# The order of work in a two-block attention kernel: from a planner that looks ahead to written strings

## The reference

```
attn = softmax((q / |q|) @ (k / |k|).T * exp(min(logit_scale, ln 100)) + bias[rel_index])
h = relu(gn1(x + proj(attn @ v)));  z = relu(gn2(h + mlp(gn(h))))
```

```
attn = softmax(q.T @ k * 16 ** -0.5);  out = w_proj @ (attn @ v) + z
```

## Time and profile before

| what | us |
|---|---|
| median of three runs | 9722.46 |
| the profiled execution | 9728.87 |
| its span, first to last instruction | 9726.9 |
| TensorE (PE) busy in it | 8771.4 |
| VectorE (DVE) busy in it | 7528.1 |
| ScalarE (ACT) busy in it | 6459.0 |
| GpSimd (POOL) busy in it | 834.0 |

### The profile page before, as it was taken

How to read it: one execution, slowest core, us unless ns; L and a number is a source line. 1 busy time by engine, 2 the same in 40 slices (tenths; PEclk the granted TensorE clock), 3 DMA queues, 4 the chain that set the end, 5 groups by cost and what they waited for, 6 DMA issues and landing times.

```text
span 9726.9 us, 373040 instructions
## 1 busy us (share of the span) xinstructions
PE 8771.4 (90%) x145926; PEld 4275.9 (44%) x145926; DVE 7528.1 (77%) x9622; ACT 6459.0 (66%) x13874; POOL 834.0 (9%) x676
## 2 busy tenths in 40 slices
PE   4799999999999999999999999999999999999997
PEld 2344444444444444444444444444444444444443
DVE  3677887777787787887778877777877878877785
ACT  1466676676766667666666766767666676666777
POOL 3000100101000000000001001010000000000000
PEclk8799999999999999999999999999999999999999
DMA  1201102020020201102011020100202011020110
GB/s 29 42 10 23 30 6 45 10 37 16 9 42 8 43 11 22 29 7 44 10 22 31 6 44 10 33 20 9 42 8 43 11 21 31 7 44 10 22 23 18
DMA packets 123195, 225.77 MB, mean 23 GB/s; under 512 B 57218, under 2 KB 89090, under 8 KB 121354
## 3 DMA queue, kind: packets, MB, share of 16 engines
q1 hardware_dynamic: 121490, 201.52, 11.5%
HBM read 67.50 MB, written 42.73 MB: 11 GB/s over the span
## 4 chain that ended last, share of the span: by engine, by line
PE 71%; DVE 12%; DMA 5%; SPq 5%; issue 4%; ACT 3%; DVEq 0%; POOL 0%; ACTq 0%; POOLq 0%
PE PS L1210 20%; PE PS L1351 20%; PE PS L1363 19%; DVE small L991 7%; PE PS L1251 3%; PE PS L1271 2%; SPq L696 2%; DMA q_stack<-neg_rows 2%; DVE small L1030 1%; ACT exps L929 1%; SPq L725 1%; PE PS L1303 1%; DVE win_scores L1033 1%; PE PS L1312 1%; DMA tok_unit<-in_query_ident 1%
## 5 line engine op out<-in xcount | busy, mean ns | idle before, releaser
L929 ACT ACTIVATE exps<-PS 128x392 f32<-128x392 f32 x12800 | 5656.2, 499 | 2602.4 <-PE PS L1351 2089.2
L991 DVE TENSOR_REDUCE small<-PS 128x1 f32<-128x784 f32 x6400 | 5912.9, 966 | 964.4 <-PE PS L1210 775.6
L1351 PE MATMUL PS<-q_stack,k_stack 99*32 99x392 bf16 x51200 | 3802.0, 338 | 181.7 <-DMA q_stack<-neg_rows 85.0
L1210 PE MATMUL PS<-k_stack,q_stack 96*32 96x392 bf16 x51200 | 3497.5, 353 | 300.8 <-DVE small L991 194.9
L1363 PE MATMUL PS<-exps,v_all 128*32 128x392 f32 x25600 | 2740.7, 500 | 34.9 <-DVE o_st L1151 27.5
L1351 PEld LDWEIGHTS PS<-q_stack,k_stack 99*32 99x32 bf16 x51200 | 1461.7, 97 | 1845.9 <-ACT exps L929 1030.4
L1210 PEld LDWEIGHTS PS<-k_stack,q_stack 96*32 96x32 bf16 x51200 | 1210.7, 99 | 2020.5 <-DVE small L991 1148.6
L1363 PEld LDWEIGHTS PS<-exps,v_all 128*32 128x32 f32 x25600 | 802.3, 111 | 331.4 <-issue 62.0
L829 POOL TENSOR_TENSOR win_scores<-win_scores,small 128x784 f32<-128x784 f32 x256 | 384.5, 1502 | 3917.4 <-DVE small L1042 3917.4
L1030 DVE TENSOR_REDUCE small<-PS 128x16 f32<-128x784 f32 x256 | 247.2, 966 | 369.2 <-PE PS L1251 369.2
L1251 PE MATMUL PS<-kmask,tok_unit 113*64 113x392 f32 (+1 forms) x2048 | 399.5, 513 | 77.3 <-DMA tok_unit<-in_query_ident 69.6
(11 more groups left out here) (113 smaller groups left out, 3030.9 us busy)
## 6 DMA issues: line engine op xcount, KB each, us to landing
q_stack<-tok_qk SPq DMA_DIRECT2D x320, 98.0 KB, 3.7
k_stack<-tok_qk SPq DMA_DIRECT2D x320, 98.0 KB, 4.2
kmask<-tok_unit SPq DMA_DIRECT2D x1024, 12.2 KB
att<-scratch_att SPq DMA_DIRECT2D x68, 196.0 KB
z_half<-scratch_z SPq DMA_DIRECT2D x34, 392.0 KB, 5.8
inv_sums<-scratch_rden SPq DMA_DIRECT2D x272, 49.0 KB, 2.1
out<-inv_sums SPq DMA_DIRECT2D x68, 196.0 KB, 2.7
scratch_att<-o_st SPq DMA_DIRECT2D x512, 26.0 KB
```

Source lines behind the costliest of these rows:

```text
L929: nc.scalar.activation(exps(u), PS[:, u % SCORE_BANKS, 0:GTOK], ACT.Exp, scale=D1 ** -0.5).then_inc(s_exps, 1)
L991: nc.vector.tensor_reduce(max_parts[:, n_:n_ + 1], slot(), op=ALU.max, axis=AX.XY)\
L1210: last = mm(PS[32 * r:32 * r + 32, it.bank + j, 0:GTOK], q_stack[0:STACK, stage // 2, q0:q0 + 32], k_stack[0:STACK, stage // 2, chunk * GT ...
L1351: last = mm(PS[32 * r:32 * r + 32, u % SCORE_BANKS, 0:GTOK], k_stack[0:STACK + SHIFT, h, k0:k0 + 32], q_stack[0:STACK + SHIFT, h, c * GTOK ...
```

## The change

The walk that tries and looks ahead (earliest_unit, Walk, start, arrange) is gone. TensorE's list is written down as a string of letters for the prologue, the loop image and the last image. `follow` reads it: TensorE takes the next letter's step, SP, ScalarE, VectorE and GpSimd what is ready first in the walk, and for VectorE a part that empties a slot before another. Costs are in ns and differ a little. LEAD is 18, so 70 maxima stand in the prologue and 330 in the last image; the loop image keeps 400. The steps, their instructions and their semaphore waits are as before. The new loop string has 116 changes of tile shape. The diff, cut: of PARTS and LAST_ORDER only the beginning or end, of the functions removed only their names.

```diff
 PARTS = {
-    "score": (("PE", 17),), "exp": (("ACT", 41),), "weigh": (("PE", 69),),
-    "max": (("PE", 34), ("DVE", 90)), "shift": (("PE", 25), ("DVE", 16), ("SP", 25)),
-    "copy": (("DVE", 51),), "store": (("SP", 32),),
...
+    "score": (("PE", 167),), "exp": (("ACT", 380),), "weigh": (("PE", 664),),
+    "max": (("PE", 334), ("DVE", 884)), "shift": (("PE", 160), ("DVE", 220), ("SP", 2260)),
+    "copy": (("DVE", 560),), "store": (("SP", 1240),),
+    "xload": (("SP", 1100),), "xorder": (("POOL", 500),),
...
-SHIFT_PIECES = 140
-TAIL = {"PE": 20, "DVE": 18, "ACT": 18, "POOL": 15, "SP": 350}
-LATE = {"stack": 1200, "xload": 800, "sums": 1500, "zload": 1500, "rden": 600, "rspread": 700}
-AHEAD, PATIENCE = 600, 40
-SWITCH, URGENT = 10, 7
+SHIFT_PIECES = 1400
+TAIL = {"PE": 225, "DVE": 140, "ACT": 165, "POOL": 110, "SP": 3500}
+LATE = {"stack": 5000, "xload": 4000, "sums": 5500, "zload": 9000, "rden": 3500, "rspread": 3000, "zstore": 4000,
+        "kload": 2500, "queries": 2500, "shift": 3000}
+SWITCH = 100
...
-MAX_LOW, MAX_START, MAX_RATE = 4, 6, 2.0
-
 MAXIMA = [(stage, tile, pair) for stage in range(STAGES) for tile in range(*STAGE_TILES[stage % 2])
           for pair in range(PAIRS)]
 MAX_INDEX = {m: n for n, m in enumerate(MAXIMA)}
 STAGE_MAXIMA = [[m for m in MAXIMA if m[0] == stage] for stage in range(STAGES)]
-LEAD = 6
+LEAD = 18
 LEAD_IN = STAGE_MAXIMA[0] + STAGE_MAXIMA[1][:LEAD]
 
...
-def earliest_unit():
...
-class Walk:
...
-    def work(self, until):
...
-def start(needs, maxima, attended, last_slots):
...
+LETTERS = {"s": "score", "W": "weigh", "M": "max", "H": "shift", "q": "qk", "u": "sum", "p": "spread", "k": "wscore",
+           "v": "wval", "t": "wtrans", "o": "wpv", "j": "wproj", "g": "gn", "a": "mlp1", "b": "mlp2", "z": "gqk",
+           "y": "gv", "F": "final"}
+PROLOGUE_ORDER = (
+    "qqqquppvkkttkkopttokkvttkkotptkkotvtjkkottjkkovttjkkottojggggaaaabbaaaabbggzzzzyyyMMMMMMMMMMMMMMMMMMMMMMMMMMMMMM"
+    "MMMMMMMMMMMMMMMMMMMMMMMMMMMMMHMMMMMMMMMMM")
+IMAGE_ORDER = (
+    "MssMsMsssMWssMsMssWMssMssMWMsssMsMssWMMssWsssMsMssWMsMssWMsssMsMWMsssMsMWMsssMsqqqqsssMWMsMMsssWuMMWMMsssHMsssWs"
+    "WssppssMWssMMsssMWMssMsssMssMWMsvskkWssspsssWMsWsssMstWMsssMstkksssWWoMMsssMsssWMstWsMsstkkssssWoMMssWssMsstvsss"
+    "MWMsstkksssWWMssMsssMWosssMMsWsMssstMssWsMktWsssMksssWssMWMsssossMWMsssMsWMssstMWsssMMssWsMssMssWMssMsWssMMsWsss"
+    "psssMWHssMssMWMsssjksWsssMWMssstssMWMsssMWMsskvWjsssMssostMssWMMWssMssMsstkksssWWsMsMsssMWMsssMMsssMWMsssWMsssMW"
+    "ssMsosssMtssMWMMWsMsstMssWMkkssWsssvWsssMssossMMsWttssMWoMsMsssMMsWMsjsjsssMsWMMsWgssMsMssWssWsgssMHsssMMsssWWMM"
+    "sssMsssMWMsssMssMWWMsssFMssWsMssMssMWgsssMMssWgsMssMWMsssMssMWssMMsWsMMsMssMssMWMWMsssMMsssMWsMssaassMsMWMMsssMW"
+    "MsssMWMsssMWMsssMMWsMsMsMsssMWMsssbssWsMsMWMsssaassWHMsssaasWsMMsWsssMMsWsssMbsMssWMsssMWMsssMsMsWMsMsssWsMMsssW"
+    "sMssMsWMsssMWMssMssMsssMWMsMssWMssMWMsssaassMWMsssMWMssMssWMsssMWMssbbsssMWssMsMWsssgMsssMWMMsssMsWsssWsMssMWMss"
+    "MsssMWgssHsMssMWssMMsWMsssMMssWssMMsssWMsszzssWMsssMWMMsssMsWsMssMsWMssMsWssMssMWsssMMssWMsssMWssMsMssWssMMsssWM"
+    "ssMWsMssMWsMMsssMWssMMssWMsssMMsssMWsMssMWsMssMWMssMssssWsssMsMWsMssMsWMsssMWMssMssMWMsssMsszzsssWWMyHsssMMssWMs"
+    "ssMWsssMMssWssMsMsWMsssMWssMMsssWMsssMWsMssMWMssMsssMssMWMssMWsMssMssMWMsssMWsssMMssWMsssMWsssMMssWssMMsssWssMWs"
+    "ssMWssMMsssWssMMssWsMssMWMsssMssMssMWMWMssyysMsssMWssMMssWMsssFHssWsMMsssWssMMsssWMMsssWMMsssWssMMsssWMsssMWsssM"
+    "MssWsMssMsWMsssMWsssMMssWsMssMsWMssMsWssMMssWsMssMWssMMsssWssMsMsWsMssMssWsssWssMsMssWsssMWssMMsssWssMHssWssMsWs"
+    "ssMMssWsMssMssWMMsssWssMMsssWssMsMWW")
+LAST_ORDER = (
+    "MMsssMsssMWMssMssMWMssMssMssWsMMssWsssMMssWsMssMsWMssMWssMssMssMWMsssMWMsssMsMssWMMsssWMssMssWsMssWsMsssMWMsssMW"
...
+    "ssMsWssMMsssWssMMsssWMssMsWssMMsssWssMMsWssWssMMsssWssMMsssWMssMssWsssWsssHssWsssWsssssWsssWsssssWssssWsssWsssss"
+    "WsssWsssssWsssWsssssWsssWsssssWsssWssssWsssssWsssWsssssWsssWsssssWsssWsssssWsssWsssssWsssWsssssWsssWsssssWW")
+
+
+def follow(needs, letters, slot=0):
+
     tasks = [(step, part) for step in needs for part in range(len(PARTS[step.kind]))]
     number = {task: n for n, task in enumerate(tasks)}
     engine = [ENGINES.index(PARTS[step.kind][part][0]) for step, part in tasks]
+    users, missing = [[] for _ in tasks], [0] * len(tasks)
     for n, (step, part) in enumerate(tasks):
         before = {(b, len(PARTS[b.kind]) - 1 if p is None else p) for b, p in needs[step]}
         for key in before if part == 0 else [(step, part - 1)]:
             users[number[key]].append(n)
             missing[n] += 1
+    steps = {kind: iter([step for step in needs if step.kind == kind]) for kind in LETTERS.values()}
+    tensor = [number[next(steps[LETTERS[letter]]), 0] for letter in letters]
+    assert len(tensor) == engine.count(0)
+    ready, free, shape, placed = [0] * len(tasks), [0] * 5, (128, 32), 0
+    offered = [[n for n in range(len(tasks)) if not missing[n] and engine[n] == e] for e in range(5)]
+    order, bank, slots, emptied = {e: [] for e in ENGINES}, {}, [None, None], {None: 0}
+    for _ in tasks:
+        choice = []
+        if placed < len(tensor) and not missing[tensor[placed]]:
+            n = tensor[placed]
+            waits = [ready[n], free[0]]
+            if tasks[n][0].kind in SLOTS:
+                waits.append(emptied.get(slots[0], 10 ** 9))
+            choice.append((max(waits), 0, n))
+        for e in range(1, 5):
+            if offered[e]:
+                first = max(free[e], min(ready[n] for n in offered[e]))
+                ranked = [(e == 1 and tasks[n][0].kind not in SLOTS, ready[n], n) for n in offered[e] if ready[n] <= first]
+                choice.append((first, e, min(ranked)[2]))
+        begin, e, n = min(choice)
+        assert begin < 10 ** 9, tasks[n]
+        step, part = tasks[n]
+        kind = step.kind
+        duration = PARTS[kind][part][1]
+        if e == 0:
+            placed += 1
+            duration += SWITCH * (SHAPE[kind] != shape)
+            shape = SHAPE[kind]
+            if kind in SLOTS:
+                bank[step] = RING_BANKS[slot % 2]
+                slot += 1
+                slots = [slots[1], step]
+        else:
+            offered[e].remove(n)
+            duration += SHIFT_PIECES * (kind == "max" and step[1:] == STAGE_MAXIMA[step.i][-1])
+        free[e] = begin + duration
+        late = free[e] + (LATE.get(kind, TAIL["SP"]) if e == 4 else TAIL[ENGINES[e]])
+        if kind in SLOTS and part == (2 if kind == "gqk" else 1):
+            emptied[step] = late
         order[ENGINES[e]].append(Entry(*step, part, bank.get(step)))
+        for user in users[n]:
+            missing[user] -= 1
+            ready[user] = max(ready[user], late)
+            if not missing[user] and engine[user]:
+                offered[engine[user]].append(user)
+    return order, slot
...
 def prologue_order():
-    needs = {**layer0_needs(False), **maxima_needs(LEAD_IN, [0])}
-    last = [at("max", *m) for m in LEAD_IN[-2:]]
-    return arrange(needs, LEAD_IN, False, 1, last)
+    return follow({**layer0_needs(False), **maxima_needs(LEAD_IN, [0])}, PROLOGUE_ORDER, 1)
 
 
 def image_order(more):
@@ -405,15 +306,14 @@
     maxima = [m for stage in range(1, STAGES) for m in STAGE_MAXIMA[stage]][LEAD:]
     needs = {**attention_needs(), **finish_needs()}
     if not more:
-        return arrange({**needs, **maxima_needs(maxima, list(range(1, STAGES)))}, maxima, True)
+        return follow({**needs, **maxima_needs(maxima, list(range(1, STAGES)))}, LAST_ORDER)
     maxima += LEAD_IN
-    needs = {**needs, **layer0_needs(True), **maxima_needs(maxima, list(range(1, STAGES)) + [0])}
-    return arrange(needs, maxima, True, 0, [at("max", *m) for m in LEAD_IN[-2:]])
+    return follow({**needs, **layer0_needs(True), **maxima_needs(maxima, list(range(1, STAGES)) + [0])}, IMAGE_ORDER)
 
 
 (PROLOGUE, FIRST_SLOT), (MORE, MORE_SLOTS), (LAST, _) = prologue_order(), image_order(True), image_order(False)
 assert FIRST_SLOT % 2 == 0 and MORE_SLOTS % 2 == 0, (FIRST_SLOT, MORE_SLOTS)
-EPILOGUE, _ = arrange(finish_needs(), [], False)
+EPILOGUE, _ = follow(finish_needs(), "FF")
```

More of the change, by code:

```diff
@@ L4 @@
 from collections import namedtuple
-from dataclasses import dataclass, replace
 IMAGES, CH, RES, WIN = 16, 64, 56, 7
@@ new lines @@
+    "relu": (("ACT", 920),), "hstats": (("DVE", 1060),), "mlp_in": (("ACT", 920),),
+    "mlp1": (("PE", 660), ("ACT", 815)), "mlp2": (("PE", 1310), ("DVE", 1150)),
+    "zrelu": (("ACT", 920),), "zstore": (("SP", 500),), "zmid": (("ACT", 450),),
+    "gqk": (("PE", 660), ("ACT", 720), ("DVE", 890)),
+    "piece_m": (("ACT", 750),), "piece_l": (("POOL", 1600),), "gv": (("PE", 890), ("DVE", 700)),
+    "stack": (("SP", 9000),), "vcopy": (("POOL", 470),),
+    "sums": (("SP", 2200),), "zload": (("SP", 500),), "srecip": (("DVE", 380),), "rden": (("SP", 650),),
@@ L201, in maxima_needs @@
     return needs
-def earliest_unit():
-    quad = {}
```

(56 more changed lines are left out.)

138 lines of the change are left out of this document (18 added, 120 removed).

## The result

The changed kernel takes 8928.22 us (median of 4 runs, 8923.68 to 8930.84), the kernel before 9723.02 beside it: a ratio of 0.9179, 95% interval 0.9165 to 0.9194. The forecast was 8605, with a range of 8350 to 8900. The time is 323 us over the forecast and close to rival A's price of 8882.

A forecast was written before the change was run, and what follows sets the result against it. TensorE (497 us need an image) and VectorE (456) were taken as close, with 95 of 592 us lost. Images of 497 + 3 + 15 + 4 = 519 save 1095: 9728.9 − 1095 − 20 − 6.4 = 8607, forecast 8605, range 8350 to 8900.

The forecast's parts named there:

- rival A: Loop images: the pieces understate VectorE's surplus, 33 us instead of 15, so image 537 us, kernel 8882; chance 0.23.
- Same work, 497 us of need: Loop image: the same steps stay, so TensorE still needs 497 us and VectorE 456; only the loss can change.
- The runs of maxima and their clock: Loop image: no more than two maxima side by side, so the long runs go and the clock becomes 0.99.
- Surplus 15 and chain waits 4, together 19 us: Loop image: 15 us where VectorE needs more than TensorE, plus 4 for waits in layer 0's chains.
- Pieces of 30 steps: Strings cut into about 10 us each to sum VectorE's surplus: 42 us in the old image, 15 in the new.
- The jump, 3 us: Loop image's start: TensorE's 3.20 us of "issue" idle ahead of the first maximum stays, counted as 3 us.
- Stack 3 in SP's queue, nothing: Image start: its DMAs issue earlier and land just ahead of q; nothing taken, 150 us kept as an end.
- Last image, 400 us: Last image: 400 us where 420 were taken, 20 us gained, ends 15 and 28.
- Prologue 0: Prologue: twelve more maxima, +12 us, against closer k steps and later p and y; 0 taken, ends −8 and +8.
- Stage boundaries: Between H and a stage's first score: the wait for row DMAs, 5.3 us an image, goes.
- rival C: Window groups: late DMAs hold k and everything behind; at 12 us an image the kernel takes 10047; chance 0.04.
- The rule that speaks against it: Image start: a gap without matmuls halves TensorE's rate; 5 us an image, 75 in all, sum 8680; not included.

The follow-up runs named there:

- run 3: The kernel before's TensorE order written as strings with 6 maxima ahead, other engines in the changed kernel's new walk; 9846.70 us, 1.0116 of the kernel before.
- run 4: Changed kernel with 6 instead of 18 maxima of stage 1 done an image ahead; 9087.81 us, 0.9336 of the kernel before.
- run 2: Changed kernel with VectorE's maximum reading only 392 of 784 columns; 8773.05 us, 0.9016 of the kernel before.
- run 8: Changed kernel with both VectorE's maximum and ScalarE's exponential over half their columns; 8569.74 us, 0.8814 of the kernel before.
- run 9: Changed kernel with only ScalarE's exponential halved, 196 of 392 columns, maxima whole; 8846.68 us, 0.9092 of the kernel before.
- Run 12: Changed kernel with three images written out, two x loads and fourth stack ahead of the denominators, and new strings spacing maxima; 8728.44 us, 0.8972.
- run 14: Changed kernel's strings, three images written out, all four x loads and the fourth stack ahead of the denominators; 8835.97 us, 0.9076 of the kernel before.
- run 13: Changed kernel, loop over single images, all four x loads and the fourth stack ahead of the denominators; 8896.72 us, 0.9139 of the kernel before.
- run 16: Changed kernel with new, slightly moved strings, loop over single images, all four x loads ahead of the denominators; 8664.52 us, 0.8902 of the kernel before.
- run 5: Changed kernel, loop over single images, VectorE's two reciprocals allowed only behind the 48th scores step; 8914.47 us, 0.9171 of the kernel before.
- Run 1: Changed kernel with three images written out, the loop running 5 times instead of 15; 8943.43 us, 0.9188 of the kernel before.

## Why the prediction was wrong

- *Same work, 497 us of need:* held. By pitches the new image needs 493.6; with both other engines relieved it is at most 502.9.
- *The runs of maxima and their clock:* held in direction. The runs and the low clock beside them are gone, and the loop gained 777 us; run 3 shows that with the new walk the whole gain hangs on TensorE's order, and run 4 that the lead is part of it. How much the runs of maxima made is not shown, for no run takes them away alone. By the calm pitches, 47 of the 95 us that an image of before loses lie in its runs of three or more M and the 20 steps behind each.
- *Surplus 15 and chain waits 4, together 19 us:* the step that failed first. The steps behind the 120th alone lose 31 us. ScalarE had no term in a loop image, though a score may lead its exponential by only three banks, as a maximum its reduction by two slots; runs 2, 8 and 9 put 9.5 us to VectorE alone, 4.5 to ScalarE alone and 8.8 to the two together. The 15 us written for VectorE lie between its 9.5 us alone and its 18.3 once ScalarE is relieved, so what the sum lacked is ScalarE and the waits that the two share. Pieces of 30 steps also let an engine lead by some 10 us, where two slots allow under 2; the text said so and took them all the same, but no run shows what this cost. Run 12 took half of the 31 away with the same steps in another order (382 single maxima for 282, 61 runs of three or more scores for 132).
- *The jump, 3 us:* the second term that was mis-sized. The image's first 60 steps lose 9.3 us. Without a jump ahead they lose 1.8 (run 14). The first gap of the earlier trace rows was read, the second one was not looked for, and the clock behind it, which the prediction named, had no term in its sum. The runs price a jump at 5.0 to 6.1 us.
- *Stack 3 in SP's queue, nothing:* right for the place named (VectorE waits 0.5 us for the stack in after's whole run), partly by luck, and wrong for the chain. The stack's issue was to start some 8 us into the image and q to come 24 us behind the first score; in the image above they come at 13 us (3078.56) and 28, both late by about as much. The last store's landing, the denominators, x and the stack end at the same time as the jump does, so each hid the other. Of the 6.6 us in steps 60 to 120, run 13 gives back 2.0; with the new strings (run 16) 1.2 are left.
- *Last image, 400 us:* 408.1; with the reciprocals behind that chain (run 5) 399.3. The chain that the loop's jump hides was bare here, and the step had no term for it. That run 5 meets the 400 is luck: by the calm pitches its tail without maxima loses 10.5 us where 14 were written, the rest 7.0 where 4 were.
- *Prologue 0:* 8.5 us gained, past the end −8. *Stage boundaries, rival C:* TensorE waits for the DMAs of k 15.7 us in the whole run, as shown above (8.8 of them in the fifteen loop images), and for those of a shift not at all.
- *Rival A:* its price was right within 50 us, in part by luck. It had 33 us of an image for what is 31 behind the 120th step, but from the two slots and the half clock alone, where ScalarE has a share; and the jump's second gap and the chain are not in it.
- *The rule that speaks against it:* the rule of the Trainium skill ("TensorE: Matmul & The Clock Gate", section on HAM oscillation) came true. The trace shows 6.8 or 10.2 us at clock 0.50 behind each jump; half of that, 3.4 to 5.1 us, is an estimate of what it costs, where the prediction had priced it at 5 and then left it out of the sum. Run 1 shows the same behind 4.77 us in which TensorE stood for VectorE.

In sum: 8605, plus 318 in the loop, 8 in the last image, less 8.5 in the prologue, plus 4 (the profiled run of before lay 6.4 us over its median, that of after 2.6): 8927, for 8928 measured. The forecast had rounded 8607 to 8605.

What stays open is how the 9.2 us behind the 120th step that no relief of VectorE and ScalarE takes away divide between waits and pitches that are a little too short, and how a jump's 5 to 6 us divide between its gaps and the clock. A loop with no jump at all was not tried.

## What to carry to other kernels

Price a rigid order step by step against the depth of its buffers (here two slots and three banks), for every engine that empties one: a sum for one engine alone misses the waits that two engines share, 8.8 us an image here. When a cost is taken away and the time stands still, list at which step the time comes back: here one trace named the next link each time, and the jump's 5 to 6 us were to be had only once the whole chain of loads behind the last store was moved. In a queue that issues in order, put a transfer that waits for a store to land behind all loads that wait for nothing; with the jump in place this gave some 30 to 40 us here (run 13: 31 by the medians, 39 by the ratios).

## What the runs showed of the hardware

- A jump back in a body of some 9000 matmuls costs TensorE two gaps, 3.44 and 2.07 us, and 5.0 to 6.1 us in all once nothing else hides it.
- Behind the jump's first gap the granted clock is 0.50 (1.2 GHz of 2.4) for 6.8 or 10.2 us; 6.8 us of it also come with a gap of 4.77 us in which TensorE stood for VectorE (run 1).
- From the issue of four stores of 26 KB (901.38) to the first load that waits for them (908.39) pass 7.0 us; 1.24 of them are the issue, and for the other 5.8 the queue stands idle.
- Half the columns are not half the time: the recorded maximum falls from 966 to 564 ns, the exponential from 500 to 333.
